# Mamba layers and a routed mixture of experts on one Trainium2 core: an expert plan cut into small pieces, the lead search moved to the last unit, and a state product put ahead of a transpose

## The chip, the core and the metric

One core of a Trainium2 chip. TensorE multiplies and transposes, VectorE, ScalarE and GpSimd do the elementwise work, SyncE issues most transfers. Each engine runs its own list of instructions in order; semaphores tie the lists together. The metric is the device time of one execution in microseconds.

## What is computed

Two Mamba2 layers on 8 sequences of 512 tokens of 256 features, a residual and a layernorm, then a mixture of 8 experts (2 per token), a residual and a layernorm. All in float32:

```python
for i in range(2):                                   # _mamba2, per layer
    res = h
    u = layernorm(h, ln_w[i], ln_b[i])
    z, xBC, dt = split(u @ in_w.T)
    dt = softplus(dt + dt_bias)
    xBC = silu(causal_conv(xBC, 4 taps) + conv_b)
    # scan over tokens, 8 heads, state 64 x 64:
    #   state = exp(dt*A)*state + (dt*x) B^T ;  y = state C
    y = (y + D * x) * silu(z)
    y = y * rsqrt(mean(y*y) + eps) * rms_w
    h = y @ out_w.T + res
x = layernorm(x + h)
logits = x @ gate_w + gate_b                         # top 2 of 8, softmax
for e: out_e = (silu(x @ w1g[e] + b1g) * (x @ w1v[e] + b1v)) @ w2[e] + b2[e]
x = layernorm(x + sum_of_two(out_e * weight))
```

## The kernel before, in words

**Units.** A unit is one sequence in one layer; units 0 to 15 follow each other (layer 0 is 0 to 7, layer 1 is 8 to 15). Each is worked in four chunks of 128 tokens. `schedule` (L142) calls, for each engine, a function with its order written out by hand: `prologue`, `first`, `plain` for units 1 to 8, `routed` for 9 to 14 (unit u also routes the tokens of sequence u - 9, whose layers ended a unit before), `final` for unit 15 and `epilogue`. Units 10 to 13 are two turns of a loop of two.

For a chunk TensorE does, among others: `chunk_cb` (C times B), `chunk_y` (the part of y within the chunk, L794, sixteen records), `chunk_z` (the old state times C, L781), `chunk_s` (the new state, L803), `chunk_c` (transposes of the gated g, L812) and `chunk_d` (output product, L830). `do_fills` puts the projections of the next unit between them. g comes from GpSimd (`gated`, L2506), which needs VectorE's `chunk_b2` (L1703), which needs `chunk_y`. `chunk_z` of chunk 1 needs ScalarE's `first_state` (L1278). VectorE's share is `scan` (L1676), `chunk_mix` (L1684), the taps of the convolution (L1637), `g_low` (L1610), the sum of layer output and residual `end_add` (L1660), and the routing (`s3_stats`, `s3_top`, `s3_place`).

**Lead search.** Each token's row is scattered by GpSimd (L2456) to a queue per expert in DRAM. `choose_lead` (L1841, eleven small VectorE instructions, each waiting for the one before) picks the expert that has most rows after six sequences. Its 6 first tiles (`NLEAD`) are worked before the counts are complete. It is issued in unit 14, behind `s3_place`. GpSimd's `first_weights` waits for it and loads that expert's 3 MB in four quarters; ScalarE (L1289) and VectorE (L2062) split them into two halves of float16.

**Expert tiles.** 71 tiles of 128 rows, in groups of three. Per tile TensorE turns the rows (`turn`, L1054, two transposes), makes four banks of 24 products (L1076: gate and value of half 0, of half 1) and the result (L1101, 24 products) of the tile before; its order is turn of tile j + 2, banks of tile j + 1, result of tile j. ScalarE takes the gate's silu (L1520) and a high part (L1526). VectorE's tile is `rows_low` (L2044), then per half `gated` (L2232) and `low_part` (L2239), with `weigh_rows` (L2052, L2055) in between; `result` of the tile before (L2263) follows the tile. `turn` of tile j waits for its rows and for `rows_low` of tile j - 1. SyncE loads rows of tile j + 3 (L518 for the first six tiles, L572 after) behind the answer of tile j - 1 (L578), that is behind VectorE's `result`. From tile 6 on, the address of the rows comes from the plan, so SyncE waits for `plan_done`.

**Plan.** VectorE counts tiles per expert (`plan_tiles`, L2119 to L2132), finds which expert each tile has (`plan_places`, L2136 to L2148), and packs words and addresses (`plan_words`, L2155 to L2173; its last cast raises `plan_done`). `step` makes the engine wait for each instruction before the next. `rows_moved` (L2177 on), `rows_of_pick` and others prepare the final gathers. They stand whole between tiles: `plan_tiles` behind tile 0, `plan_places` behind tile 1, `plan_words` behind tile 2, `rows_moved` behind tile 3.

**GpSimd behind the units.** For experts 1 to 7: `load_weights` (four quarters; those of expert 1 are issued at once, later ones one after another) and `split` (L2406 to L2408, fifteen instructions). It waits for `plan_done` ahead of the load of expert 2.

## Time and profile before

| | before |
|---|---|
| median of three runs | 1465.58 us (1463.50 to 1468.26) |
| profiled execution | 1464.89 us, of it 1462.9 us span |
| TensorE busy | 1309.9 us, 90% |
| VectorE busy | 1110.9 us, 76% |
| ScalarE, GpSimd busy | 797.7 and 802.3 us, 55% each |
| mean of what the transfers moved | 99 GB/s over the span |

Times in the rows are microseconds from the start of the span. A matmul's end is modelled, and matmuls overlap a little, so a group of a bank shows 1.52 us where the next begins after 1.36. The granted clock of TensorE has two levels here, 1.2 and 2.4 GHz; a mean between them tells of a stretch with both. An idle time in brackets stands with the engine that ended it, as the semaphores show.

### The profile page before, as it was taken

To read this page: it belongs to the slowest core of one execution; us is meant where nothing else is said; L and a number is where in the kernel's file an instruction comes from. 1 tells how busy PE (TensorE), PEld (TensorE's weight loads), DVE (VectorE), ACT (ScalarE), POOL (GpSimd) and SP (SyncE) were. 2 spreads that over 40 slices of the span, in tenths; PEclk is the share of its full clock that TensorE was granted. 3 is DMA by queue.
4 is the path that set the end of the run, shared out by engine and by line. 5 is a ranking of instruction groups with operands and counts; after the bars stand their busy time and mean duration, and the time that the engine had idled before them with its cause. 6 is when DMAs were issued, how large, how long until landed. Compare 5 with 4: busy or idle time off the path is not lost.

```text
span 1462.9 us, 39961 instructions
## 1 busy us (share of the span) xinstructions
PE 1309.9 (90%) x13112; PEld 1038.5 (71%) x13113; DVE 1110.9 (76%) x2564; ACT 797.7 (55%) x1821; POOL 802.3 (55%) x738
## 2 busy tenths in 40 slices
PE   3889999999999999999888699999999999999970
PEld 1456665656666566566657589999999999999970
DVE  4889999999999898899877976656565656565537
ACT  4657666666576566566545245444444444444434
POOL 3466767766776777687775601506061607152771
PEclk9999999999999899899867899999999999999985
DMA  5313443223343233312415230212203222202594
GB/s 175 110 29 116 131 129 100 90 99 116 116 131 116 77 113 113 119 59 102 151 63 158 95 125 29 93 54 75 72 29 120 76 70 63 88 29 61 137 204 150
DMA packets 94655, 145.72 MB, mean 100 GB/s; under 512 B 13488, under 2 KB 77488, under 8 KB 94448
## 3 DMA queue, kind: packets, MB, share of 16 engines
q1 hardware_dynamic: 79216, 97.06, 21.0%
q0 software_dynamic: 15072, 46.51, 10.7%
q10 hardware_dynamic: 288, 1.19, 0.2%
q8 instruction: 39, 0.64, 0.2%
q14 instruction: 40, 0.33, 0.1%
HBM read 103.06 MB, written 41.67 MB: 99 GB/s over the span
## 4 chain that ended last, share of the span: by engine, by line
PE 58%; DVE 19%; issue 9%; POOL 8%; ACT 4%; DMA 1%; SPq 1%; DVEq 0%; ACTq 0%; POOLq 0%
PE pe L1076 13%; PE pa L1076 12%; PE py L1101 12%; PE pa L659 4%; DVE arena L1637 3%; POOL arena L2506 3%; PE pm L830 3%; PE pa L651 3%; PE py L794 3%; DVE arena L1676 2%; PE pz L781 2%; PE pt L812 2%; DVE arena L1684 1%; DVE arena L1703 1%; POOL arena L2496 1%
## 5 line engine op out<-in xcount | busy, mean ns | idle before, releaser
L1076 PE MATMUL pe<-arena 128*128 128x128 f16 x3408 | 222.9, 222 | 19.4 <-issue 17.4
L1076 PEld LDWEIGHTS pe<-arena 128*128 128x128 f16 x3408 | 207.2, 99 | 24.3 <-issue 21.4
L1076 PE MATMUL pa<-arena 128*128 128x128 f16 x3408 | 219.4, 220 | 2.1 <-issue 2.1
L1520 ACT ACTIVATE arena<-pe,arena 128x128 f32<-128x128 f32 x568 | 162.1, 371 | 83.4 <-PE pe L1076 81.9
L1076 PEld LDWEIGHTS pa<-arena 128*128 128x128 f16 x3408 | 201.9, 98 | 2.2 <-issue 2.2
L1101 PE MATMUL py<-arena 128*128 (+1 forms) x1704 | 197.5, 273 | 0.8 <-DVE arena L2263 0.8
L1637 DVE SCALAR_TENSOR_TENSOR arena<-pa,arena 128x511 f32<-128x511 f32 (+2 forms) x240 | 178.7, 745 | 8.1 <-ACT arena L1172 1.8
L1101 PEld LDWEIGHTS py<-arena 128*128 128x128 f16 x1704 | 163.5, 98 | 18.8 <-issue 1.1
L2406 POOL TENSOR_SCALAR arena<-arena 128x1536 f16<-128x1536 f32 (+2 forms) x35 | 42.7, 1220 | 216.2 <-DVE arena L2263 202.6
L2232 DVE SCALAR_TENSOR_TENSOR pm<-pa,arena 128x128 f32<-128x128 f32 x284 | 80.4, 352 | 98.0 <-ACT arena L1520 85.0
L794 PEld LDWEIGHTS py<-arena 128*128 128x128 f32 x1024 | 128.7, 202 | 35.5 <-issue 21.8
L1676 DVE TENSOR_TENSOR_SCAN arena<-arena,pe 128x512 f32<-128x512 f32 x128 | 148.7, 1203 | 3.4 <-issue 2.0
L794 PE MATMUL py<-arena 128*128 128x64 f32 x1024 | 133.8, 287 | 0.6 <-DVE arena L1684 0.6
L651 PE MATMUL pa<-arena 128*128 128x512 f16 x480 | 120.5, 391 | 3.6 <-DVE arena L1637 2.4
L2506 POOL TENSOR_TENSOR arena<-arena 128x512 f32<-128x512 f32 x64 | 88.7, 1386 | 63.0 <-DVE arena L1703 62.8
L1526 ACT ACTIVATE arena<-pm 128x512 f16<-128x512 f32 x71 | 42.4, 597 | 131.3 <-DVE pm L2232 131.3
L830 PE MATMUL pm<-arena 128*128 128x256 f16 x768 | 103.0, 288 | 8.6 <-DVE arena L1610 8.1
L2232 DVE SCALAR_TENSOR_TENSOR pz<-pa,arena 128x128 f32<-128x128 f32 x284 | 80.4, 351 | 39.6 <-ACT arena L1520 38.6
L1526 ACT ACTIVATE arena<-pz 128x512 f16<-128x512 f32 x71 | 42.4, 597 | 109.6 <-DVE pz L2232 109.6
L830 PEld LDWEIGHTS pm<-arena 128*128 128x128 f16 x768 | 78.3, 104 | 32.2 <-DVE arena L1610 10.1
L659 PE MATMUL pa<-arena 128*128 128x512 f16 x384 | 97.3, 396 | 4.2 <-ACT arena L1161 2.0
L2676 POOL DMA_INDIRECT arena<-answer,arena x64 | 61.6, 963 | 57.9 <-issue 57.6
(297 smaller groups left out, 2557.8 us busy)
## 6 DMA issues: line engine op xcount, KB each, us to landing
arena<-step_rows SPq DMA_DIRECT2D x64, 512.0 KB, 6.3
arena<-in_w_exp POOLq DMA_DIRECT2D x32, 768.0 KB, 4.7
arena<-queue SPq DMA_DIRECT2D x74, 129.5 KB, 2.1
answer<-arena SPq DMA_DIRECT2D x71, 128.0 KB, 1.7
arena<-in_x SPq DMA_DIRECT2D x16, 512.0 KB, 6.7
answer<-zeros SPq DMA_DIRECT2D x10, 512.0 KB, 4.8
arena<-h SPq DMA_DIRECT2D x9, 512.0 KB, 6.3
h<-arena SPq DMA_DIRECT2D x8, 512.0 KB, 3.0
```

The lines of the kernel that those rows point to most:

```text
L651: ins = pe.matmul(bank[:, :], win[:, l, b, d, OX + c * P:OX + (c + 1) * P], uT[:, vq, a, d, :], start=(n == 0), stop=(n == len(passes) - 1))
L659: ins = pe.matmul(bank[:, :], uT[:, vq, a, d, k * P:(k + 1) * P], win[:, l, b, d, 0:DI], start=(n == 0), stop=(n == len(passes) - 1))
L794: ins = pe.matmul(py[:, h * HD:(h + 1) * HD], mix[:, kq, h, :], dtx[:, kq, h, :], start=True, stop=True)
L830: ins = pe.matmul(OUT, gT[:, c.kq, a, t, :], wout[:, c.layer, b, t, :], start=(n == 0), stop=(n == len(passes) - 1))
L1076: ins = pe.matmul(bank[:, f * P:(f + 1) * P], w_split[:, p, hl, d * 2 * FF + col:d * 2 * FF + col + P], x[:, r, d, :], start=(n == 0), sto ...
L1101: ins = pe.matmul(py[:, 0:D], a[:, b, f, :], part(p, hl, W1N + f * D, D), start=(half == 0 and n == 0), stop=(half == 1 and n == len(passe ...
L1520: ins = e.activation(sg[:, half, f, :], GATE[half][:, f * P:(f + 1) * P], ACT.Silu, bias=b1a[:, bass.ds(ex_, 1), ff], scale=1.0 / S1)
L1526: e.activation(acth[:, r, 4 * half:4 * half + 4].rearrange("p f t -> p (f t)"), GLU[half][:, :], ACT.Copy).then_inc(hi_done[half], 1)
L1637: ins = dve.scalar_tensor_tensor(acc[:, mq, s:T], pa[bank][:, 0:T - s], cw[:, l, ct, TAPS - 1 - s:TAPS - s], acc[:, mq, s:T], ALU.mult, AL ...
L1676: dve.tensor_tensor_scan(flat[:, h * T:(h + 1) * T], step_b[:, c.k, h * T:(h + 1) * T], IDENT4[:, :], 0.0, ALU.mult, ALU.add).then_inc(sca ...
L2232: ins = dve.scalar_tensor_tensor(GLU[half][:, f * P:(f + 1) * P], VALUE[half][:, f * P:(f + 1) * P], b1v[:, bass.ds(ex_, 1), ff], sg[:, ha ...
L2506: pool.tensor_tensor(g[:, kq], y2[:, kq], zs[:, c.q, k].rearrange("p (h d) -> p h d", h=NH), ALU.mult).then_inc(g_ready, 1)
```

## The change

Four edits.

1. In `routed`, TensorE issues `chunk_z` of chunk 1 ahead of `chunk_c` of chunk 0 (six units).
2. VectorE issues `choose_lead` in `final` behind `chunk_mix` of chunk 1 and ahead of `end_add`, no longer in unit 14. In GpSimd's `final`, `first_weights` and the first scatter come behind `gated`, `x_w`, `x_dt` and `old_state`, no longer in front.
3. The plan's three functions become ten, with the same instructions in the same order but for one (`row_f` is made a little earlier). They stand between the halves of a tile or between tiles, from tile 0 to tile 4, and the last, `plan_out`, behind the result of tile 3. What follows (`rows_moved`, picks, needs) comes two tiles later, and VectorE's loop starts at group 4 instead of 3.
4. GpSimd waits for `plan_done` behind the load of expert 1 and ahead of its split; the four quarters of expert 1 are issued one after another.

```diff
@@ TensorE, routed @@
                 chunk_cb(c[2])
+                chunk_z(c[1])
                 chunk_c(c[0])
-                chunk_z(c[1])
                 chunk_y(c[1])
@@ VectorE, routed @@
                 s3_place(st, ch3)
-                if isinstance(st.u, int) and st.u == NB + BEFORE_LEAD:
-                    choose_lead()
                 scan(c[4])
@@ VectorE, final @@
                 chunk_mix(c[1])
+                choose_lead()
                 end_add(st)
@@ VectorE, the plan @@
-            def plan_tiles():
+            def count_tiles():
...
+            def tiles_by_place():
...
+            def ends_of_places():
...
-            def plan_places():
+            def places():
...
+            def experts_of_tiles():
...
+            def starts_of_tiles():
...
+            def parities():
...
-            def plan_words():
+            def words():
...
+            def rows_of_tiles():
...
+            def plan_out():
...
+                step(dve.tensor_reduce(plan_f[0:1, 3 * NJT + 2 * NE:], usedj[0:1, 0:NJ].rearrange("p (g r) -> p r g", r=WB),
+                                       AX.X, ALU.add))
                 dve.tensor_copy(plan_i[0:1, :], plan_f[0:1, :]).then_inc(plan_done, 1)
@@ VectorE, tiles @@
+            def first_half(i, r, ex_, expert):
+                rows_low(i, r + 1)
+                gated(i, r, 0, ex_)
+                weigh_rows(i, r + 1, expert)
+                low_part(i, r, 0)
+
+            def second_half(i, r, ex_):
+                gated(i, r, 1, ex_)
+                low_part(i, r, 1)
@@ VectorE, order @@
-            tile(0, 0, first, lead[:, 0:1])
-            plan_tiles()
-            tile(0, 1, first, lead[:, 0:1])
+            first_half(0, 0, first, mine)
+            count_tiles()
+            second_half(0, 0, first)
+            tiles_by_place()
+            first_half(0, 1, first, mine)
+            ends_of_places()
+            second_half(0, 1, first)
             result(0, 0, True)
-            plan_places()
-            tile(0, 2, first, lead[:, 0:1])
+            places()
+            first_half(0, 2, first, mine)
+            experts_of_tiles()
+            second_half(0, 2, first)
             result(0, 1, True)
-            plan_words()
-            tile(1, 0, first, lead[:, 0:1])
+            starts_of_tiles()
+            first_half(1, 0, first, mine)
+            parities()
+            second_half(1, 0, first)
             result(0, 2, True)
+            words()
+            first_half(1, 1, first, mine)
+            rows_of_tiles()
+            second_half(1, 1, first)
+            result(1, 0, False)
+            plan_out()
+            first_half(1, 2, first, e_tab[:, NLEAD:NLEAD + 1])
+            second_half(1, 2, first)
+            result(1, 1, False)
             rows_moved()
...
-            with dve.Fori(3, NGRP) as i:
+            with dve.Fori(4, NGRP) as i:
@@ GpSimd, load_weights @@
-                    if n > 0 and e > 1:
+                    if n > 0 and e > 0:
                         pool.wait_ge(w_raw_in, 16 * (4 * e + n))
@@ GpSimd, final @@
                 end(st)
-                first_weights()
-                scatter_before(st, 0, 1)
                 gated(c[0])
                 x_w(c[1])
                 x_dt(c[1])
                 old_state(c[1])
+                first_weights()
+                scatter_before(st, 0, 1)
                 scatter_before(st, 1, 3)
@@ GpSimd, behind the units @@
                     pool.wait_ge(w_have, 1)
-                if e == 2:
+                load_weights(e)
+                if e == 1:
                     pool.wait_ge(plan_done, 1)
-                load_weights(e)
```

## Rows read from the trace of the kernel before

**Rows 1.** The page: TensorE's granted clock in 40 slices, tenths of 2.4 GHz
```profile
PEclk9999999999999899899867899999999999999985
```

**Rows 2.** Windows of two routed units: busy time and count, clock, DMA
```profile
485.37:537.26 51.89, 49.71 (x294) 32.63 (x293) 43.39 (x110) 31.18 (x63) 37.00 (x37) 0.87 0.32 103
...
636.69:683.62 46.93, 44.84 (x294) 29.99 (x293) 43.23 (x110) 31.17 (x63) 37.05 (x37) 0.96 0.30 101
```

**Rows 3.** Timeline of TensorE, units 10, 12, 14: start, us, instruction, [idle before, releaser]
```profile
487.06 0.65 PE L812 MATMUL pt<-ident,arena 128*128 128x128 f32 x4 [1.20 <-POOL arena L2506]
487.64 2.07 PE L781 MATMUL pz<-arena 64*128 64x512 f32 x2
...
588.31 1.11 PE L812 MATMUL pt<-ident,arena 128*128 128x128 f32 x4 [3.64 <-POOL arena L2506]
...
685.77 1.12 PE L781 MATMUL pz<-arena 64*128 64x512 f32 x2
```

**Rows 4.** Timeline of VectorE, the lead search and the last unit's sum
```profile
716.93 1.04 DVE L1850 TENSOR_TENSOR lead_score<-count,qbase 128x8 f32<-128x8 f32 x1
...
721.94 0.17 DVE L1860 CAST at_pos<-lead_pos 128x8 int32<-128x8 f32 x1
...
737.25 1.57 DVE L1660 TENSOR_TENSOR arena<-arena 128x1024 f32<-128x1024 f32 x1 [3.32 <-ACT arena L1240]
```

**Rows 5.** Timeline of TensorE, last output product of unit 14
```profile
724.99 2.74 PE L830 MATMUL pm<-arena 128*128 128x256 f16 x12 [5.78 <-DVE arena L1610]
```

**Rows 6.** Windows, four microseconds in the last unit
```profile
728.00:732.00 4.00, 4.00 (x20) 3.67 (x20) 1.18 (x2) 0.15 (x1) 0.15 (x1) 0.50 1.02 419
```

**Rows 7.** Timeline of TensorE, turns of rows (L1054) and a first bank, early tiles
```profile
815.71 0.66 PE L1054 MATMUL pt<-ident,arena 128*128 128x128 f32 x2 [4.46 <-DMA arena<-queue]
816.16 2.72 PE L1076 MATMUL pe<-arena 128*128 128x128 f16 x24
...
835.52 0.66 PE L1054 MATMUL pt<-ident,arena 128*128 128x128 f32 x2 [9.94 <-issue]
...
847.52 0.41 PE L1054 MATMUL pt<-ident,arena 128*128 128x128 f32 x2 [1.82 <-DMA arena<-queue]
...
856.55 0.38 PE L1054 MATMUL pt<-ident,arena 128*128 128x128 f32 x2
...
864.83 0.38 PE L1054 MATMUL pt<-ident,arena 128*128 128x128 f32 x2
```

**Rows 8.** Timeline of VectorE, plan functions (L2119, L2136, L2155 to L2173) and tiles (L2044)
```profile
796.49 0.34 DVE L2119 TENSOR_SCALAR arena<-jrow 128x32 f32<-128x32 f32 x1
...
800.77 0.42 DVE L2044 TENSOR_TENSOR arena<-pt,arena 128x256 f16<-128x256 f32 x1
...
806.84 0.78 DVE L2136 TENSOR_TENSOR arena<-jrow,arena 128x600 f32<-128x600 f32 x1
...
812.72 0.42 DVE L2044 TENSOR_TENSOR arena<-pt,arena 128x256 f16<-128x256 f32 x1
...
818.78 2.95 DVE L2155 COPY arena<-arena 1x25 f32<-1x25 f32 x1
...
833.82 1.27 DVE L2173 CAST arena<-arena 1x244 int32<-1x244 f32 x1
```

**Rows 9.** Timeline of SyncE's DMA issues, early tiles
```profile
807.57 0.35 SPq L518 DMA_DIRECT2D arena<-queue  x1
...
843.20 0.35 SPq L572 DMA_DIRECT2D arena<-queue  x1
```

**Rows 10.** Timeline of GpSimd, last unit and split of expert 1
```profile
723.79 2.30 POOL L2390 DMA_DIRECT2D arena<-in_w_exp  x4 [1.22 <-issue]
...
747.00 0.20 POOL L2446 TENSOR_TENSOR arena<-arena 128x4 f32<-128x4 f32 x1
...
818.60 3.10 POOL L2408 TENSOR_TENSOR arena<-arena 128x1536 f16<-128x1536 f32 x1
```

**Rows 11.** Timeline of ScalarE, split of expert 0's weights (high parts)
```profile
756.72 1.48 ACT L1289 ACTIVATE arena<-arena 128x1536 f16<-128x1536 f32 x1
```

More of the change, by code:

```diff
@@ L2115, in _ @@
             par_f = plan_f[0:1, 2 * NJT:3 * NJT]
-            def plan_tiles():
+            NG = NJT // WB
+            number, odd = pos_j[0:1].rearrange("p (g r) -> p g r", r=WB), ej[0:1].rearrange("p (g r) -> p g r", r=WB)
+            packed = par_f[:, 0:NG]
+            def count_tiles():
                 step(dve.tensor_scalar(j128, jrow[:, 0:NTILE], float(P), None, ALU.mult))
@@ L2166, in plan_words @@
                 dve.tensor_copy(plan_f[0:1, 3 * NJT + NE:3 * NJT + 2 * NE], end[0:1, :])
+                step(dve.tensor_tensor(row_f, tmpj[0:1], jd, ALU.add))
+            def plan_out():
                 step(dve.tensor_tensor(usedj[0:1, 0:NJ], jrow[0:1, 0:NJ], end[0:1, NE - 2:NE - 1].to_broadcast([1, NJ]),
                                        ALU.is_lt))
[L2170 to L2172 removed]
+                step(dve.tensor_reduce(plan_f[0:1, 3 * NJT + 2 * NE:], usedj[0:1, 0:NJ].rearrange("p (g r) -> p r g", r=WB),
+                                       AX.X, ALU.add))
                 dve.tensor_copy(plan_i[0:1, :], plan_f[0:1, :]).then_inc(plan_done, 1)
@@ L2241, in low_part @@
                                   ALU.subtract).then_inc(act_done, 1)
-            def tile(i, r, ex_, expert):
-                rows_low(i, r + 1)
-                for half in range(2):
-                    gated(i, r, half, ex_)
-                    if half == 0:
-                        weigh_rows(i, r + 1, expert)
-                    low_part(i, r, half)
+            def first_half(i, r, ex_, expert):
[6 more added lines that the diff above has]
+                low_part(i, r, 1)
+            def tile(i, r, ex_, expert):
+                first_half(i, r, ex_, expert)
+                second_half(i, r, ex_)
             def planned(i, r):
```

25 lines of the change are left out of this document (11 added, 14 removed).

## The prediction

> **What bounds the kernel now.** I read the page first for where TensorE is not at full clock: slices 14 and 17, 20 to 23, and the last two [rows 1]. The last two are the tail, which the change doesn't touch. So I read three stretches: the routed units (430 to 720 us), the last unit (720 to 783), and the first expert tiles (783 to 858).
>
> Routed units, each measured from its `chunk_cb` of chunk 2: unit 13 (636.69 to 683.62) lasts 46.93 us, VectorE busy 43.23 and TensorE 44.84; unit 10 lasts 51.89 [rows 2]. Both engines are near full, so what one gains the other may take back. In all six routed units TensorE waits over 1 us for GpSimd's g ahead of the transposes L812. In units 10 and 12 that wait (1.20 and 3.64 us) is followed by half clock: the state product L781 takes 2.07 us where it takes 1.12 in unit 14 [rows 3].
>
> Last unit: the search for the leading expert stands in VectorE's order ahead of unit 14's last scan. It starts at 716.93 and its last step ends at 722.11: 5.2 us for eleven tiny steps [rows 4]. TensorE idles 5.78 us behind it, comes back at 1.2 GHz [rows 5] and stays there though it is busy, 4.00 us of 4.00 in 728 to 732 at 0.50 [rows 6].
>
> Early tiles: TensorE waits 4.46, 9.94 and 1.82 us ahead of its turns of tiles 4, 5 and 6 [rows 7]. The first is for rows whose load was issued at 807.57 and used at 815.71 [rows 7, 9]; the second for VectorE, which sits in `plan_words` from 818.78 to 835.09 [rows 8]; the third for a load issued at 843.20 [rows 9]. In steady state a tile costs TensorE 8.28 us, turn to turn [rows 7], and VectorE 6.07 (800.77 to 806.84) [rows 8]. From there on the program is TensorE's, and answers, gathers and the final normalisation follow counts of tiles, so a time saved before that is saved at the end.
>
> **Part 1, state product ahead of the transposes (six units).** The product needs only `first_state`, long done when TensorE stands waiting. At full clock its 1.05 us (1.12 less overlap) fits into the waits; the transposes start no later. In units 9, 11, 13 and 14, however, TensorE later waits for VectorE's taps anyway, so it hands back what it won; I take 0, bounds 0 and 1 us for the four. Unit 10 is 51.89 - 46.93 = 5.0 us longer than unit 13 [rows 2]. If the filled wait keeps the clock, all of it comes back; if the clock falls all the same, the path is still shorter by one product at half rate, 2.0. I take 4.0. In unit 12 a wait of 3.64 - 1.05 = 2.6 us is left, so the clock falls as before, and the product is off the path: 2.0, less what VectorE's order takes; 1.5. A fall could also move to another place, where it costs 3 to 5 us, so the bounds are -3 and 8. Part 1: 5.5 us.
>
> **Part 2, the search moved.** In unit 14 the 5.2 us go from in front of the scan, so `g_low` of chunk 3 is ready at about 719.8 and TensorE idles 0.8 us, as much as in the units before (0.3 to 1.0). Then its clock should hold. Its work from 724.99 to the end of the state's product at 734.5 is 9.5 us without a wait at half clock, so 4.7 at full: that product ends near 725.0. ScalarE's first state, rows and scaling (3.2 us) let `end_add` begin near 728 instead of 737.25 [rows 4]. Now the search stands right in front of it, behind `chunk_mix` of chunk 1, which ends near 725.2. There VectorE waited 3.32 us for ScalarE before [rows 4]; of the search's 2 to 5 us some 2.8 are hidden, and it sets `end_add` back by 0 to 2.4, taken as 1.3. VectorE would be some 8 us ahead.
>
> GpSimd has more to do in that stretch. Its issue of expert 0's weights (723.79, 2.30 us) [rows 10] and the scatter behind it lay in idle time. Now they stand behind the old state, in the middle of work without a gap: x_w at 726.1, three products to 729.2, weights to 731.8, three scatters to 735.7, two products to 738.1, then the root at 739.4 instead of 747.2 [rows 10]: 7.8 ahead. That is the chain which the trace shows critical in this unit, so GpSimd's 7.8 counts, not VectorE's 8. The weights land about 8.4 us after their last issue, near 740; ScalarE's split of the first quarter began at 756.72 [rows 11], so near 748 after: hidden by 8 us. If the clock stays at half, only the 5.2 less the search's new 1.3 remains, about 3.5. I take 7.5, bounds 1 and 9.
>
> **Part 3, the plan in ten pieces.** The same instructions are issued, with one wait more. Until the plan is handed out VectorE has 4.3 us (796.49 to 800.77), 5.9 (806.84 to 812.72) and `plan_words`, whose 15 instructions took 16.3 us [rows 8]. The first two show such steps at 0.2 to 0.3 each, so 3.8 is the size of the third alone. What makes it 16.3: a copy of 1x25 lasts 2.95 us [rows 8], until a GpSimd subtraction begun at 818.60 ends [rows 10]; GpSimd splits expert 1 just then. The change keeps the split back until the plan is out, so the plan is 4.3 + 5.9 + 3.8 = 14.0 us. The Trainium skill ("SBUF — State Buffer", on its doors and the shared port pair) says that a GpSimd operation and a VectorE operation that is in a two-port mode or has two SBUF inputs exclude each other for the whole instruction. By that rule taken literally the sum would be rival A's below; these two rows agree with it.
>
> When is the plan out? VectorE leaves tile 0 at 796.49 [rows 8], then 14.0 of plan and four tiles of 6.07: 834.8, less 1 us of ScalarE waits that pieces between halves cover: 834. Before it was 835.09. So the plan is out no sooner; but tile 4 is done by then, where tile 2's result was open.
>
> TensorE: turn 3 as before. Turn 4's rows need `result(0,0)`, behind the same 4.3 us, so they are issued at 807; their 8.1 us fell among four weight quarters in flight at once, now one at a time, and the load at 843.20, beside single quarters, took 4.2 [rows 7, 9]. So turn 4 near 811.4, waiting 0 to 0.5 (4 if it stays 8.1). Turn 5 waits for VectorE's lag, about 0.6. Turn 6 is asked for at 811.4 + 0.6 + 2 x 8.28 = 828.6, and gets its rows only from the plan: 834 + 1.3 (SyncE's waits and address) + 2.6 (a load beside no weights, issued at 800.11 and used at 802.78) = 837.9. That is a new wait of 9.3 us, for plan, SyncE and DMA. The clock falls; the first bank behind such a gap took 2.72 for 1.52 [rows 7], and with a second and the turn that is 1.6. Old turn 6: 847.52 at full clock. Gain: 847.5 - 837.9 - 1.6 = 8.0.
>
> Given back: expert 1's split (25.5 us) ran from 815.5 and now runs from 834 to 860, over `rows_moved` and the first `rows_of_pick`. At the rate of `plan_words` (1.09 us an instruction) `rows_moved`'s eight cost 8.7 instead of 1.5. VectorE has 2.2 us of slack a tile and had just been waiting for TensorE at turn 6, so of these 7 us TensorE sees some 1; bounds 0 and 7. TensorE needs expert 1 at tile 11, after 885. Part 3: 7.0, bounds 1 and 9.
>
> Sum: 5.5 + 7.5 + 7.0 = 20.0. The profiled execution took 1464.89 (span 1462.9 and 2.0 around it), 0.7 under the median 1465.58. 1465.6 - 20.0 = **1445.6**.
>
> **The rivals.**
> - A, the lock moves with the split. For this rival every blockable step of `rows_moved` (seven of eight) and of the first pick (three of four) waits for a whole GpSimd instruction. For: the copy of 2.95 us [rows 8]. Against: 15 steps passed in the time of 10 GpSimd instructions, so half the time two pass at one boundary. Part 3 gives 1: 1451.6. Chance 0.20.
> - B, VectorE and GpSimd take the gain of the units. Clock falls only move, and the last unit stays at 1.2 GHz. For: 43.2 of 46.9 us busy [rows 2]. Part 1 gives 0, part 2 gives 3.5: 1465.6 - 10.5 = 1455.1. Chance 0.14.
> - C, both: 1 + 3.5 + 0: 1461.1, within 0.3%. Chance 0.09.
> - D, slower: after turn 6's wait the clock does not come back for several tiles (tiles 5 to 8). For: 1.2 GHz held with TensorE busy 4.00 of 4.00 us [rows 6]. Against: after waits of 4.46 and 9.94 it came back within two banks. A tile at half clock costs 8.3 more; from 2.4 tiles on the 20 us are gone, four give 1465.6 - 20 + 33 = 1479. Chance 0.06.
> - E, the change does not do what it says for the search: another expert leads, or first weights come late. Against: the search sees the same counts (unit 14's are the last added at both places), and the margin is 8 us. Time as without part 2: 1453.1. Chance 0.03.
>
> **How the numbers follow.** Forecast 0.48, its own range 1441 to 1450. A, B and E are faster too. About 0.3% (4.4 us) is what a measurement can tell from no change. Faster: 0.48 + 0.20 + 0.14 + 0.03 = 0.85, of which 0.02 moves to same, as B adjoins it: 0.83. Same: 0.09 + 0.02 = 0.11. Slower: 0.06. Range: from 1439 (all three parts at their upper bounds, 26 us, is 1439.6) to 1460, which takes in A, B and E and leaves out C and D, 0.15, and an edge of B.
>
> **What would show it.** Right: 722 to 747 at full clock and the root near 739; no wait over 2 us at turns 4 and 5, one of 8 to 10 us at turn 6, ended by a load issued just after the plan's last cast; expert 1's split starting at that cast and `rows_moved` stretched; unit 10 near 47 us. Wrong: turn 4 still waiting 4 us (the quarters were not its cause); unit 10 at 52; TensorE waiting behind `rows_moved` for over 3 us.

## The result and the profile after

| | before | after |
|---|---|---|
| median | 1465.71 us (1463.50 to 1468.26, four runs) | 1444.99 us (1442.04 to 1445.83, four runs) |
| ratio | | 0.9854, 95% interval 0.9833 to 0.9876 |
| profiled execution | 1464.89, span 1462.9 | 1445.83, span 1443.9 |
| TensorE busy | 1309.9 | 1300.4 |
| VectorE busy | 1110.9 | 1098.9 |

1445.6 was forecast. The page of the changed kernel, TensorE's granted clock in 40 slices:

```profile
PEclk9999999999999999999967999999999999999985
```

Against [rows 1], slices 14 and 17 are at full clock now; the dip in the last unit is still there, as 6 and 7 in slices 21 and 22.

To place the difference I cut both traces at the same instructions: the first `steps` product of units 9 and 14 (L764, weights `tri_le`), the first bank of tile 0, and the turns of tiles 10 and 13.

| stretch | before | after | gain | forecast |
|---|---|---|---|---|
| start to unit 9 | 437.71 | 439.88 | -2.2 | 0 |
| units 9 to 13 | 245.13 | 233.15 | 12.0 | 5.5, with unit 14 |
| unit 14 and last unit, to tile 0's first bank | 100.23 | 98.27 | 2.0 | 7.5 |
| tile 0's first bank to turn 10 | 99.29 | 92.36 | 6.9 | 7.0 |
| the rest | 580.5 | 580.2 | 0.3 | 0 |

The sum is 19.0, the difference of the spans, for a forecast of 20.0. So the total is right, and two of its terms are not. The first line is code that the change leaves alone; the last section returns to it.

**Units.** The windows of all five units, before and then after (columns as in [rows 2]):

```profile
437.71:682.84 245.13, 231.60 (x1467) 154.37 (x1466) 217.46 (x547) 156.05 (x310) 179.66 (x175) 0.93 0.31 101
```

```profile
439.88:673.03 233.15, 219.52 (x1467) 148.55 (x1466) 216.62 (x547) 156.50 (x310) 179.48 (x175) 0.98 0.33 107
```

TensorE is busy 12.1 us less at a clock of 0.98 for 0.93, and its idle time is the same (13.5 and 13.6 us). By estimate from these two clocks, 17 us of full-speed work were lost to half clock before and 5 after, which is the whole 12. VectorE is busy only 0.8 us less, so VectorE's gain must be waits. Its waits in those units before (who waited, for whom: us in all, times, longest):

```profile
DVE arena L1710 <- PE pz L803: 6.1, 5, 3.4
DVE pe L1813 <- PE pa L704: 4.4, 4, 1.3
...
DVE arena L1703 <- PE py L794: 1.8, 2, 0.9
DVE arena L1690 <- PE pz L781: 1.4, 2, 0.7
```

It had waited for TensorE too: for the new state (L1710), for the ranks of the routing (L1813), for the chunk's products. Of these 13.7 us, 9.9 lie in units 10 and 12; units 9, 11 and 13 have 1.5, 1.1 and 1.2, nearly all of it for the ranks. The prediction took VectorE as an engine that TensorE waits for in these units, not the other way round.

Units 9, 11 and 13 were not undisturbed before, either: each has a stretch of some 3 us at half clock. Unit 13 before, that stretch of it, and unit 13 after:

```profile
635.90:682.84 46.94, 44.85 (x295) 30.00 (x294) 43.24 (x111) 31.18 (x62) 36.94 (x36) 0.96 0.30 101
662.00:664.00 2.00, 2.00 (x8) 0.83 (x7) 2.00 (x4) 0.60 (x1) 1.70 (x3) 0.50 1.02 382
```

```profile
627.38:673.03 45.65, 43.09 (x295) 29.04 (x294) 43.21 (x111) 31.38 (x62) 36.85 (x36) 1.00 0.31 105
```

**Last unit.** TensorE, VectorE and GpSimd of the changed kernel, timeline (start, us, engine, line, instruction, [idle before, releaser]):

```profile
710.64 1.47 PE L830 MATMUL pm<-arena 128*128 128x256 f16 x12 [0.31 <-ACT arena L1232]
...
731.11 2.07 PE L781 MATMUL pz<-arena 64*128 64x512 f32 x2 [4.21 <-DVE arena L1710]
733.11 3.58 PE L692 MATMUL pa<-arena 128*128 128x8 f32 x16
...
739.47 3.68 PE L794 MATMUL py<-arena 128*128 128x64 f32 x16
```

```profile
729.77 0.69 DVE L1703 TENSOR_TENSOR arena<-py,arena 128x512 f32<-128x512 f32 x1 [1.44 <-POOL arena L2542]
730.38 0.67 DVE L1710 TENSOR_TENSOR arena<-pz,arena 64x512 f32<-64x512 f32 x1
```

```profile
720.93 2.28 POOL L2436 DMA_DIRECT2D arena<-in_w_exp  x4
723.52 1.05 POOL L2502 DMA_INDIRECT queue<-arena  x1 [0.30 <-issue]
...
726.19 0.96 POOL L2502 DMA_INDIRECT queue<-arena  x1 [0.31 <-issue]
727.17 1.05 POOL L2530 TENSOR_TENSOR arena<-arena 128x512 f32<-128x512 f32 x1
728.38 1.26 POOL L2542 TENSOR_TENSOR arena<-arena 128x512 f32<-128x512 f32 x1 [0.15 <-POOL arena L2530]
...
730.73 0.20 POOL L2492 TENSOR_TENSOR arena<-arena 128x4 f32<-128x4 f32 x1
```

The wait of 5.78 us in [rows 5] is 0.31 us now, the clock is full up to 727, and the root's last step stands at 730.73, counted from unit 14's start 6.5 us ahead of its old place in [rows 10] (7.8 forecast). Up to the last output product of unit 14 (L830, 710.64) this is a gain of 4.5 us, 37.6 for 42.2. But the weights and three scatters (720.93 to 727.2) now stand ahead of x*d and its sum (727.17 to 729.6). VectorE's `chunk_b2` of chunk 1 (L1703) waits 1.44 us for that sum, the new state (L1710) is behind it, and TensorE waits 4.21 us for the state. From L830 to tile 0's first bank TensorE takes 60.7 us for 58.1 before, so 2.6 of the 4.5 are lost again. TensorE is back at half clock, with L781 at 2.07 and L794 at 3.68 us, busy all the time:

```profile
731.00:745.00 14.00, 13.89 (x46) 9.54 (x46) 5.05 (x7) 4.14 (x9) 8.59 (x8) 0.50 0.21 78
```

**Early tiles.** TensorE's turns 5 and 6 (L1054) and the banks behind turn 6; then two of VectorE's steps of the plan, its last among them, and SyncE's load for tile 6:

```profile
809.08 0.41 PE L1054 MATMUL pt<-ident,arena 128*128 128x128 f32 x2 [1.30 <-DMA arena<-queue]
...
823.72 0.66 PE L1054 MATMUL pt<-ident,arena 128*128 128x128 f32 x2 [6.18 <-DMA arena<-queue]
824.17 2.77 PE L1076 MATMUL pe<-arena 128*128 128x128 f16 x24
826.73 1.97 PE L1076 MATMUL pa<-arena 128*128 128x128 f16 x24
```

```profile
811.37 0.15 DVE L2170 COPY arena<-arena 1x25 f32<-1x25 f32 x1
...
820.17 0.28 DVE L2193 CAST arena<-arena 1x244 int32<-1x244 f32 x1
```

```profile
821.55 0.35 SPq L572 DMA_DIRECT2D arena<-queue  x1
```

The waits of 4.46 and 9.94 us at turns 4 and 5 in [rows 7] are 0 and 1.30, and the one at turn 6 is 6.18 for 1.82. The copy of 1x25 that took 2.95 us in [rows 8] takes 0.15.

### The profile page after: what moved, and what is told of

The parts are those of the page before. It is cut to its first block, busy times and chain, and to the rows that moved or that the text cites. A ratio compares the mean times of both kernels' runs of the same rounds, so it can differ in the third digit from the quotient of the medians.

```text
span 1443.9 us, 39948 instructions
## 1 busy us (share of the span) xinstructions
PE 1300.4 (90%) x13112; PEld 1033.6 (72%) x13113; DVE 1098.9 (76%) x2564; ACT 797.2 (55%) x1821; POOL 801.1 (55%) x738
## 3 DMA queue, kind: packets, MB, share of 16 engines
q0 software_dynamic: 15072, 46.51, 11.0%
## 4 chain that ended last, share of the span: by engine, by line
PE 54%; DVE 21%; issue 10%; POOL 7%; ACT 3%; DMA 1%; SPq 1%; DVEq 1%; POOLq 0%; ACTq 0%
PE pe L1076 12%; PE pa L1076 12%; PE py L1101 11%; DVE arena L1637 3%; PE pa L659 3%; POOL arena L2552 3%; DVE arena L1676 3%; PE pa L651 3%; PE py L794 2%; PE pm L830 2%; PE pt L812 2%; PE pz L781 1%; DVE arena L1703 1%; DMA arena<-queue 1%; DVE arena L1684 1%
## 5 line engine op out<-in xcount | busy, mean ns | idle before, releaser
L1076 PE MATMUL pe<-arena 128*128 128x128 f16 x3408 | 222.1, 222 | 18.2 <-issue 17.2
L1076 PEld LDWEIGHTS pe<-arena 128*128 128x128 f16 x3408 | 206.1, 99 | 23.5 <-issue 21.7
L1076 PE MATMUL pa<-arena 128*128 128x128 f16 x3408 | 219.7, 220 | 2.2 <-issue 2.0
L1076 PEld LDWEIGHTS pa<-arena 128*128 128x128 f16 x3408 | 202.2, 98 | 2.5 <-issue 2.1
L794 PEld LDWEIGHTS py<-arena 128*128 128x128 f32 x1024 | 125.8, 199 | 30.2 <-issue 16.0
L794 PE MATMUL py<-arena 128*128 128x64 f32 x1024 | 130.3, 282 | 0.9 <-DVE arena L1684 0.9
L830 PE MATMUL pm<-arena 128*128 128x256 f16 x768 | 98.0, 279 | 5.1 <-DVE arena L1610 4.6
L830 PEld LDWEIGHTS pm<-arena 128*128 128x128 f16 x768 | 75.7, 101 | 26.6 <-issue 8.2
```

The source lines that it names most:

```text
L794: ins = pe.matmul(py[:, h * HD:(h + 1) * HD], mix[:, kq, h, :], dtx[:, kq, h, :], start=True, stop=True)
L830: ins = pe.matmul(OUT, gT[:, c.kq, a, t, :], wout[:, c.layer, b, t, :], start=(n == 0), stop=(n == len(passes) - 1))
L1076: ins = pe.matmul(bank[:, f * P:(f + 1) * P], w_split[:, p, hl, d * 2 * FF + col:d * 2 * FF + col + P], x[:, r, d, :], start=(n == 0), sto ...
```

## The experiments

Six kernels take one part alone or take one part out, two change what the trace pointed to, the last four ran side by side: the changed kernel again and three more. In the table "units" is 9 to 13, "last" from unit 14 to tile 0's first bank, "tiles" from there to the turn of tile 13 (the expectations call it turn 12, counting from the turn behind that first bank as zero; their other turns are named as here). The three stretches come from one profiled execution of each, the medians from several. Kernels p1 to p4 ran on one chip, where before had 1470.76; a1, a2, b1 and b2 on another (1473.18), the last four on a third (1468.44). The kernel before ran from 1462 to 1480 us in its 40 executions there, the longer ones at a lower mean clock (0.94 for 0.95), so a median can differ from before by more than two profiles do: p1_swap by 14.8 us in the medians and by 8.9 in the profiled spans.

| kernel | units | last | tiles | median | ratio to before, 95% |
|---|---|---|---|---|---|
| before | 245.1 | 100.2 | 124.9 | 1465.71 | |
| after | 233.2 | 98.3 | 118.0 | 1444.99 | 0.985 (0.983 to 0.988) |
| p1_swap | 233.0 | 102.1 | 125.3 | 1455.98 | 0.988 (0.984 to 0.993) |
| p2_lead | 246.2 | 97.9 | 122.6 | 1464.49 | 0.997 (0.993 to 1.000) |
| p3_plan | 246.2 | 107.6 | 118.6 | 1467.61 | 0.997 (0.994 to 1.000) |
| p4_hold | 245.1 | 100.3 | 117.7 | 1462.42 | 0.994 (0.991 to 0.998) |
| a1_free_split | 231.8 | 98.5 | 129.3 | 1456.57 | 0.990 (0.985 to 0.995) |
| a2_quarters | 232.1 | 98.3 | 122.0 | 1447.33 | 0.982 (0.976 to 0.987) |
| b1_pool_order | 231.8 | 94.7 | 119.7 | 1443.95 | 0.981 (0.976 to 0.986) |
| b2_rows_first | 231.8 | 98.1 | 118.6 | 1440.86 | 0.978 (0.973 to 0.983) |
| after_again | 233.1 | 99.3 | 119.2 | 1444.81 | 0.983 (0.978 to 0.987) |
| b3_order_again | 232.5 | 94.1 | 119.1 | 1443.49 | 0.983 (0.979 to 0.987) |
| b4_both | 233.1 | 96.1 | 115.4 | 1439.53 | 0.980 (0.976 to 0.985) |
| c1_whole_plan | 233.1 | 98.0 | 117.5 | 1441.98 | 0.981 (0.977 to 0.985) |

Behind the turn of tile 13 all fourteen profiles take the same, 554.2 to 556.0 us to the end of the span: the prediction's ground that "a time saved before that is saved at the end" holds.

### The exchange in the routed units alone: p1_swap

```diff
@@ TensorE, routed, on the kernel before @@
                 chunk_cb(c[2])
+                chunk_z(c[1])
                 chunk_c(c[0])
-                chunk_z(c[1])
                 chunk_y(c[1])
```

> The kernel before with one edit: in the routed units the state product of the second chunk goes ahead of the transposes of g. Everything else is as before. Theory (the routed units keep what TensorE's wait gave up, because VectorE was waiting for TensorE's ranks in each unit too): units 9 to 13 together are about 12 us shorter, the time falls by 10 to 13 us. Rival (the term of the prediction: VectorE takes it back, only the two disturbed units gain): 5.5 us, units 9, 11 and 13 as long as before (46.9 us).

Measured: 1455.98 for 1470.76, a little more than the 10 to 13 us expected, and units 9 to 13 took 232.95 us for 245.13: 44.94, 46.51, 45.66, 50.22 and 45.62 each. All five are shorter, those that took 46.9 before by 1.3 to 1.9. VectorE's waits in them, in the same view:

```profile
DVE arena L1710 <- PE pz L803: 2.1, 1, 2.1
...
DVE pe L1813 <- PE pa L704: 1.2, 1, 1.2
```

They fell from 6.1 and 4.4 us to 2.1 and 1.2, and the two for L1703 and L1690 (1.8 and 1.4) are off the list, whose least is 0.5: some 10 of the 12.2 us. The last stretch was 1.9 us longer than before; unit 14 up to its last output product took 42.1 us as before, so it has no share. The rival, that VectorE takes the gain back, falls. The exchange is over half of the whole change.

How much of it is order and how much clock can be told from all profiles. In the four kernels without the exchange (before, p2_lead, p3_plan, p4_hold) none of the twenty units 9 to 13 has a granted clock of 1.00; in the ten profiles with it 34 of 50 have. At the same clock of 0.96 unit 9 took 46.9 us without it and 46.2 with it (after_again), unit 13 46.9 and 46.3 (b3_order_again); at 1.00 they take 44.9 and 45.6. So against the 46.9 us of before, 0.6 to 0.7 come at the same mean clock, and another 0.7 to 1.3 where no half clock is left. That the order is what keeps the clock is shown by this count; why it fell where it did is not.

### The search moved alone: p2_lead

```diff
@@ VectorE, routed, on the kernel before @@
                 s3_place(st, ch3)
-                if isinstance(st.u, int) and st.u == NB + BEFORE_LEAD:
-                    choose_lead()
@@ VectorE, final @@
                 chunk_mix(c[1])
+                choose_lead()
                 end_add(st)
@@ GpSimd, final @@
-                first_weights()
-                scatter_before(st, 0, 1)
                 gated(c[0])
                 x_w(c[1])
                 x_dt(c[1])
                 old_state(c[1])
+                first_weights()
+                scatter_before(st, 0, 1)
```

> The kernel before with one edit: the leading expert is sought in the last unit, and GpSimd issues the weights and the first scatter behind the products of the old state. Theory: TensorE's wait of 5.8 us before the transposed decays goes, but VectorE's second half of chunk 1 waits for GpSimd's add of x*d, TensorE then waits over 3 us for the next state and runs its next banks at half clock: the time falls by 1 to 3 us only. Rival (the prediction's term): 7.5 us.

Measured: ratio 0.9965, some 5 us, for 1 to 3 expected and 7.5 by the rival; but the stretch that the edit touches gained only 2.3 (97.92 for 100.23: 5.0 won up to unit 14's last output product, 2.7 lost behind it), and another 2.3 came in the tiles, where turn 4 already stood 2.0 us nearer to tile 0's first bank (30.7 for 32.6). The same sum holds up VectorE again, by the same time, and TensorE waits 1.69 us for the state, where over 3 were expected, with half clock behind it:

```profile
738.80 0.69 DVE L1703 TENSOR_TENSOR arena<-py,arena 128x512 f32<-128x512 f32 x1 [1.44 <-POOL arena L2495]
739.41 0.67 DVE L1710 TENSOR_TENSOR arena<-pz,arena 64x512 f32<-64x512 f32 x1
```

```profile
740.13 2.07 PE L781 MATMUL pz<-arena 64*128 64x512 f32 x2 [1.69 <-DVE arena L1710]
```

The forecast 7.5 for this part is refuted. The wait for the sum of x*d comes with the edit. Half clock came once ahead of it too (L830 took 2.77 us at 733.55), which in after it did not.

### The plan's part alone: p3_plan

```diff
@@ on the changed kernel: the exchange and the search undone @@
-                chunk_z(c[1])
                 chunk_c(c[0])
+                chunk_z(c[1])
...
+                if isinstance(st.u, int) and st.u == NB + BEFORE_LEAD:
+                    choose_lead()
                 scan(c[4])
...
```

> The changed kernel with the two other parts undone: the plan in pieces, the split of expert 1 held until the plan is done, the quarters one by one; routed units and the search as before. Theory, and the prediction's term: the stretch from the first bank of tile 0 to the turn of tile 10 is about 7 us shorter than before (93.5 to 95 us for 99), and the time falls by 6.5 to 7.5 us. If the three parts are not independent (the later start of the tiles moves the loads), it falls by less than 5 or more than 9.

Measured: the tiles did what was expected, 92.8 us from the first bank to turn 10 for 99.3, so 6.5. Yet the median fell by 3.2 only, by the ratio 4.7. The difference is in the stretch ahead of the tiles, which the kernel has word for word as before: 107.57 us for 100.23. Of these 7.3 us, 5.5 came in unit 14. Its wait of 1.08 us for g, as long as before, was followed by half clock here, as in unit 10 in [rows 3]; before, L781 at this place took 1.12 us:

```profile
685.60 2.04 PE L781 MATMUL pz<-arena 64*128 64x512 f32 x2
687.57 3.67 PE L794 MATMUL py<-arena 128*128 128x64 f32 x16
...
730.35 2.74 PE L830 MATMUL pm<-arena 128*128 128x256 f16 x12 [4.85 <-DVE arena L1610]
```

From unit 14's start to that last product, this kernel and then before:

```profile
682.66:730.35 47.69, 41.36 (x223) 26.97 (x221) 39.59 (x110) 25.73 (x51) 33.28 (x33) 0.85 0.24 81
```

```profile
682.84:724.99 42.15, 34.87 (x223) 23.64 (x221) 39.99 (x110) 25.75 (x51) 33.17 (x34) 0.98 0.29 92
```

Behind it 1.8 us more came, at a clock of 0.64 for 0.68. Why the clock fell in unit 14 this time is not settled. What is shown: the same code in the same order costs 7 us more or less by where the clock is low.

### The split held, the plan uncut: p4_hold

```diff
@@ GpSimd, on the kernel before @@
-                    if n > 0 and e > 1:
+                    if n > 0 and e > 0:
...
-                if e == 2:
-                    pool.wait_ge(plan_done, 1)
                 load_weights(e)
+                if e == 1:
+                    pool.wait_ge(plan_done, 1)
```

> The kernel before with one edit: the split of expert 1 on GpSimd is held until the plan is done, and the quarters of expert 1 are started one by one; the plan is not cut. If GpSimd's split is what stretched the plan's small steps (the 1x25 copy of 2.95 us beside a pass of the split of 3.10 us), the steps of the words take 0.15 to 0.4 us, the plan's cast ends 8 to 12 us earlier than in the kernel before, and this alone gives 4 to 8 us of part 3. Rival: what counts is the cut of the plan; then the time is within 2 us of before, because the whole plan still stands between two casts of rows and TensorE waits at turns 5 and 6 as before.

Measured: tiles 117.7 us, 7.2 less than before and as good as after (118.0), so the rival, that the cut is what counts, falls. The words and the cast, whole, between two tiles:

```profile
820.89 0.16 DVE L2155 COPY arena<-arena 1x25 f32<-1x25 f32 x1
...
823.50 0.24 DVE L2170 TENSOR_REDUCE arena<-arena 1x3 f32<-1x72 f32 x1
...
823.92 0.28 DVE L2173 CAST arena<-arena 1x244 int32<-1x244 f32 x1
```

They ran from 820.89 to 824.20, in 3.3 us, where they took 16.3 in [rows 8] and the prediction had 3.8. The cast stands 38.7 us behind tile 0's first bank; in the changed kernel it is 48.9, in the kernel before 50.8. So the held split and the single quarters give the whole gain of this part, and the cut puts the cast back by ten.

### The changed kernel with the split free: a1_free_split

```diff
@@ GpSimd, on the changed kernel @@
+                if e == 2:
+                    pool.wait_ge(plan_done, 1)
                 load_weights(e)
-                if e == 1:
-                    pool.wait_ge(plan_done, 1)
```

> The changed kernel with one part undone: the split of expert 1 isn't held until the plan is done, so it runs beside the pieces of the plan. Theory (held split is what keeps the plan's small steps short): single steps of the words take 1 to 3 us again, the cast comes 4 to 9 us later than in the changed kernel, TensorE waits 10 to 15 us at turn 6 instead of 6.2, and the time is 3 to 8 us above the changed kernel. Rival (the pieces are spread so widely that the split costs nothing): within 1 us of it.

Measured: tiles 129.3 us, 11.3 more than after and 4.4 more than before. The cut and the single quarters without the held split are a loss: TensorE waits 17.58 us at turn 6, above the 10 to 15 expected, and the span is 8.7 us longer than after's, for 3 to 8. VectorE's steps, with GpSimd's instructions in the same microseconds:

```profile
822.60 1.02 DVE L2184 COPY arena<-arena 1x8 f32<-1x8 f32 x1
...
827.35 0.99 DVE L2193 CAST arena<-arena 1x244 int32<-1x244 f32 x1
```

```profile
822.56 1.04 POOL L2453 TENSOR_SCALAR arena<-arena 128x1024 f32<-128x1024 f32 x1
...
827.05 1.15 POOL L2454 TENSOR_TENSOR arena<-arena 128x512 f16<-128x512 f32 x1
```

The copy of eight elements ends at 823.62, with GpSimd's pass begun at 822.56; it took 0.16 with no split about. The cast took 0.99 for 0.28, and ended with the subtraction begun at 827.05. The Trainium skill ("SBUF — State Buffer", on the shared port pair) says that a GpSimd instruction which holds the pair keeps out for its whole length a VectorE instruction that wants it; those ends agree, to 0.02 and 0.14 us. GpSimd's spans are rough, so no more can be read from them. Not every step was held: the reduction ahead of the cast took 0.24 us beside the split too.

### The quarters at once: a2_quarters

```diff
@@ on the changed kernel @@
-                    if n > 0 and e > 0:
+                    if n > 0 and e > 1:
```

> The changed kernel with one part undone: the four quarters of expert 1's second matrix are started at once. Theory: the row loads of tiles 4 and 5 land later beside them, TensorE waits 3 to 6 us more at these turns (0.0 and 1.3 in the changed kernel), of which turn 6 takes back nothing because the plan's steps follow the tiles: 2 to 5 us above the changed kernel. Rival (turn 6 hangs on the plan alone and swallows the waits ahead of it): within 1 us.

Measured: tiles 122.0 us for 118.0 and 119.2 in the two executions of after, so 2.8 to 4.0 more; the median is 2.3 to 2.5 above after's, but on another chip, and by the ratio to before the two do not differ (0.982 for 0.985 and 0.983), so for the whole time this is not shown. Turn 4 waits 2.19 us where it waited 0, turn 5 not at all, and turn 6 stands 55.2 us behind tile 0's first bank, for 52.4 and 53.4. Starting the quarters one by one is worth some 3 us of the tiles in these profiles; that they were the cause of turn 4's wait stands, though not all of its 4.46.

### GpSimd's order in the last unit: b1_pool_order

```diff
@@ GpSimd, final, on the changed kernel @@
                 old_state(c[1])
-                first_weights()
-                scatter_before(st, 0, 1)
-                scatter_before(st, 1, 3)
                 x_d(c[1])
                 add_xd(c[1])
+                first_weights()
                 rsqrt_x1(st)
-                scatter_before(st, 3, 4)
+                scatter_before(st, 0, 4)
```

> The changed kernel with GpSimd's order in the last unit changed: x*d and its add for chunk 1 go ahead of the issue of the weights and of the scatters. Theory (this add is what VectorE's second half of chunk 1 waited 1.44 us for, TensorE 4.21 us for the next state behind it, and then the clock fell to half): TensorE's wait shrinks below 2.5 us or goes, the clock stays full to the first tile, the first bank of tile 0 comes 4 to 7 us earlier and the time is 3 to 6 us below the changed kernel. Rival (another input sets that wait, VectorE's own work ahead of it): the wait moves to the next input, and the gain is under 1.5 us.

Measured: the last stretch took 94.7 us for 98.3 (the median is 1.0 below after's, on another chip), and VectorE no longer waits for the sum (L1703 at 722.30 has no idle time ahead of it). TensorE:

```profile
715.46 1.97 PE L674 MATMUL pa<-ident,arena 128*128 128x128 f32 x8 [1.28 <-DVE arena L1660]
...
726.30 1.12 PE L781 MATMUL pz<-arena 64*128 64x512 f32 x2 [0.36 <-DVE arena L1710]
...
731.67 1.12 PE L812 MATMUL pt<-ident,arena 128*128 128x128 f32 x4 [1.55 <-POOL arena L2552]
```

The wait for the state is 0.36, for 4.21. A fall of the clock came all the same, but earlier (L674 took 1.97 us at 715.46): 0.51 from 715 to 725, 0.91 to 729, 0.50 to 735 and 0.84 to 745, by windows of this run. The 44 us ahead of tile 0 were at 0.69, for 0.59. So the cause named for the wait is right, and the stretch is 3.6 us shorter here; the next kernel, with the same order, did not keep that. That the clock would stay full to the first tile was wrong. Behind it a new wait of 1.55 us for GpSimd's gated product shows.

### The row numbers first: b2_rows_first

```diff
@@ VectorE and SyncE, on b1_pool_order @@
+            def rows_out_first():
+                dve.tensor_copy(plan_i[0:1, 0:NJT], row_f).then_inc(rows_known, 1)
...
             starts_of_tiles()
             first_half(1, 0, first, mine)
-            parities()
+            rows_of_tiles()
             second_half(1, 0, first)
+            rows_out_first()
             result(0, 2, True)
-            words()
             first_half(1, 1, first, mine)
-            rows_of_tiles()
+            parities()
             second_half(1, 1, first)
             result(1, 0, False)
+            words()
             plan_out()
+            rows_moved()
...
             result(1, 1, False)
-            rows_moved()
...
-            sp.wait_ge(plan_done, 1)
+            sp.wait_ge(rows_known, 1)
```

> The kernel of the run before this one, and the plan's row numbers are worked out ahead of its words: they are cast in the pass of tile 3, with a semaphore of their own for SyncE's loads, and the parities, the words and the moved rows follow. Theory: the load for tile 6 no longer waits for the last cast (821.55 in the changed kernel), and TensorE's wait of 6.2 us at turn 6 shrinks to 0 to 3 us: 3 to 6 us below the run before. Rival: the parities and words behind it make the split and the weights of expert 1 late, and the gain is back by turn 10: within 1 us of the run before.

Measured: the median is 3.1 us below b1's, of four runs each, and the intervals overlap. The wait at turn 6 went altogether, and turn 7 stood 59.8 us behind tile 0's first bank, for 63.1 in b1. By turn 13 1.0 us of the 3.3 was left. TensorE's idle times behind turn 6:

```profile
819.90 2.74 PE L1077 MATMUL pe<-arena 128*128 128x128 f16 x24 [2.28 <-issue]
...
845.88 0.41 PE L1055 MATMUL pt<-ident,arena 128*128 128x128 f32 x2 [1.30 <-DVE arena L2044]
...
866.38 0.41 PE L1055 MATMUL pt<-ident,arena 128*128 128x128 f32 x2 [1.57 <-DMA arena<-queue]
```

So at this place the wait for rows was first in a row of late things: a bank at 819.90 waited 2.28 us for a cause which the trace does not name and came back slow, and later turns waited for VectorE and for rows. The last unit took 98.1 us, for 94.7 in the same code of b1. It had gone into that stretch without b1's early fall, had its wait of 5.04 us for GpSimd's gated product, behind the weights and four scatters, and had half clock from there:

```profile
724.20 1.12 PE L782 MATMUL pz<-arena 64*128 64x512 f32 x2 [1.40 <-DVE arena L1711]
...
732.25 1.12 PE L813 MATMUL pt<-ident,arena 128*128 128x128 f32 x4 [5.04 <-POOL arena L2558]
```

### Four side by side

The changed kernel again:

> The changed kernel itself, unchanged, on the chip of the three runs beside it: it is what they are measured against. Expected 1444 to 1448 us, and the same three waits as in its first profile: over 4 us for the next state of chunk 1 in the last unit, about 6 us at turn 6, about 1.5 us at turn 9.

Measured: 1444.81, with waits of 4.21 us for the state, 5.79 at turn 6 and 1.58 at turn 9. Turn 3 waited 3.94 where it waited 0.80 in the first profile: these loads vary by some microseconds from one execution to the next.

The third order of GpSimd:

```diff
@@ GpSimd, final, on b1_pool_order @@
                 add_xd(c[1])
+                x_dt(c[2])
+                gated(c[1])
                 first_weights()
                 rsqrt_x1(st)
-                scatter_before(st, 0, 4)
-                x_dt(c[2])
-                gated(c[1])
                 x_w(c[2])
                 x_d(c[2])
                 old_state(c[2])
                 add_xd(c[2])
+                scatter_before(st, 0, 2)
                 gated(c[2])
...
```

> The changed kernel with GpSimd's last unit in a third order: x*d, its add, and also the gated product of chunk 1 go ahead of the issue of the weights, and the scatters go into GpSimd's idle time later. The first other order (add ahead, gated product behind) took the wait for the next state from 4.21 us to 0.36 and 1.40 us, but left one of 1.55 and 5.04 us for the gated product. Theory (GpSimd's queue in this stretch is the bound, and only an order that meets both dates gives the time): neither wait is over 1.5 us, the clock stays full to the first tile, tile 0's first bank comes 4 to 8 us earlier than in the changed kernel, counted from the last routed unit, and the time falls by 4 to 7 us. Rival (what the stretch lasts is set by whether the clock happens to be granted, or by VectorE): under 2 us.

Measured: the last stretch took 94.1 us for 99.3, so 5.2; the median fell by 1.3 only, less than these runs vary. No wait for GpSimd is left in 720 to 735, but one of 1.67 us for the state, and the clock fell behind that one too:

```profile
724.88 1.91 PE L781 MATMUL pz<-arena 64*128 64x512 f32 x2 [1.67 <-DVE arena L1710]
726.72 3.58 PE L692 MATMUL pa<-arena 128*128 128x8 f32 x16
```

Both theory and rival are half right. This stretch took 98.3 and 99.3 us in the two profiles of after, and 94.7, 98.1, 94.1 and 96.1 in the four with the sum ahead of the issues (b1, b2, b3, b4): the order is worth 0 to 5 us there, and the clock's fall no order of GpSimd removed.

The third order with the row numbers first:

> The kernel with the third order, with the plan's row numbers cast ahead of its words as in the earlier run of that edit, where the wait at turn 6 went (6.2 to 0 us) but waits and slow banks at turns 7 to 11 came in its place. Theory (the split and the tiles' own weights set the end of this stretch, not turn 6): the time from the first bank of tile 0 to turn 12 stays within 1 us of the kernel with the third order alone, and so does the whole. Rival (the waits behind it were chance): 3 us below it.

Measured: 1439.53, the lowest median of all, with tiles at 115.4 for 119.1. The rival is the nearer here, 3.7 us in the tiles, where b2 had kept 1.0 of such a gain over b1; so what the late split gives back stays open. Against after on the same chip it is 5.3 us, and the two intervals (0.976 to 0.985 and 0.978 to 0.987) overlap, so this is likely better and not shown.

All parts, but the plan uncut:

```diff
@@ on p4_hold: the exchange and the search as in p1_swap and p2_lead @@
```

> The kernel before with the exchange in the routed units, the search moved to the last unit and the split of expert 1 held until the plan is done, its quarters one by one, but with the plan in its old four blocks and not cut. Theory (the held split is what gave the time in the early tiles, the cut gave none): the stretch from tile 0's first bank to turn 12 lasts 117 to 119 us as in the changed kernel (117.95), and the whole is within 1.5 us of it. Rival (the cut gives the gain together with the later split): 4 to 7 us above the changed kernel.

Measured: 1441.98 for 1444.81, 2.8 below where 1.5 either way was expected, with overlapping intervals; tiles 117.5 for 119.2. The cast begins at 808.07, 38.8 us behind tile 0's first bank (769.32). TensorE then waits at turns 3 to 8 (1.77, 0.88, 2.09, 1.16, 0.51 and 3.33 us) where after has one long wait; two of them:

```profile
810.07 0.41 PE L1054 MATMUL pt<-ident,arena 128*128 128x128 f32 x2 [2.09 <-DMA arena<-queue]
...
841.70 0.41 PE L1054 MATMUL pt<-ident,arena 128*128 128x128 f32 x2 [3.33 <-DMA arena<-queue]
```

The rival, that the cut is what gives the gain, falls. Ten pieces, a changed loop and a second function for each half tile bring nothing that the moved wait does not bring alone.

## Why the prediction came out right, point by point

- **Part 1: 12.0 us for 5.5.** The step that failed is "TensorE later waits for VectorE's taps anyway, so it hands back what it won; I take 0". For unit 10, 4.0 were forecast and it gained 5.4 (51.89 to 46.53 between `steps`), unit 12 gained 2.1 for 1.5; those two were a little under-sized. But units 9, 11 and 13 gained 1.9, 1.3 and 1.3 where 0 stood, 4.5 in all, and the bound of 1 us for four units was too low as well. Before, TensorE waited 0.3 us for the taps in each of them (L674), and VectorE waited 0.9 to 1.3 us for TensorE's ranks; with the exchange TensorE's wait for taps is 1.1 to 1.2 us, so it does hand something back, and the one for the ranks is gone. Nor was unit 13 the undisturbed measure that it was taken for: its clock is 0.96 in [rows 2], and that stretch at half clock went too (p1_swap has the shares). A busy share near full (43.2 of 46.9 us) had been taken for an engine that waits for no one. The rival B, by which VectorE and GpSimd take the gain, falls with it.
- **Part 2: 2.0 us for 7.5.** What is asked of VectorE and the search came as written: the search took 3.0 us (715.93 to 718.96), the wait of 5.78 went, the root moved by 6.5 for 7.8. The failed step is "That is the chain which the trace shows critical in this unit, so GpSimd's 7.8 counts". The prediction had counted the weights and scatters ahead of "two products to 738.1", and saw only what stands behind them on GpSimd, the root. It did not ask who waits for those two products: VectorE's second half of chunk 1 does, TensorE's state behind it, and there the clock fell (4.21 us and L781 at 2.07 us). With the sum ahead of the issues the stretch gives back 3.6 and 5.2 us in b1_pool_order and b3_order_again, but 3.2 in b4_both and 0.2 in b2_rows_first. So the wait is the cause of a part of the missing 5.5; how large a part changes with the clock and is not settled. The bound of 1 us held.
- **Part 3: 6.9 us for 7.0, by the mechanism forecast, with two sizes off that cancel.** Turn 4 waits for nothing (0 to 0.5 forecast), turn 5 1.30 for 0.6, turn 6 stands 52.4 us behind tile 0's first bank for 54.8, and its wait is 6.2 for 9.3, because the cast was done at 49.2 for 50.9. Behind the slow banks, at turn 7, the gain was 10.3 for 8.0. The load was issued 1.1 us behind the cast and used 2.2 later (1.3 and 2.6 forecast), the next banks took 2.77 and 1.97. The split began at 820.55, at the cast's end; `rows_moved` took 5.0 us for 8.7 forecast and 1.5 before, and TensorE's waits behind it were 0.2 to 0.4 us, 1.35 for rows at turn 9, and 0.3 and 0.8 behind that. By turn 10, 3.4 us were given back for 1 forecast; the waits add up to 3.3, which is the size that the prediction named as a sign of being wrong. That 6.9 meets 7.0 is luck. That the held split is the source is shown by a1_free_split against after, and by p4_hold and c1_whole_plan, where nothing else in the early tiles stands beside it but the single quarters (some 3 us by a2_quarters). The held split with the quarters at once and the plan whole was not tried. What the prediction did not ask is whether the cut has a share: it has none, or one below nothing.
- **The sum.** Part 1 gave 6.5 more and part 2 5.5 less than forecast, and the two cancel; the 2.2 us ahead of unit 9 work against both. That 1445.6 and 1444.99 lie 0.6 apart is chance. Rival A, the lock moved with the split, falls by turn 10 and by `rows_moved`; rival D, half clock for several tiles behind turn 6, by L1076 at 1.53 us from 829.11 on. C, with 1461.1, falls by the time, and E by ScalarE's split of the first weights, which began at 744.53 with no wait (near 748 forecast).

## What to carry to other kernels

- A busy share says nothing of who waits for whom. Before an engine is taken to hand a gain back, list its own waits in that stretch and their releasers: 13.7 us stood there for VectorE, with TensorE's name. And before a stretch is taken as the undisturbed measure, look at its clock: 0.96 was not 1.00.
- When instructions are moved forward in a queue past others, name the consumer of each instruction they are put ahead of, not only the last. Six microseconds of issues stood ahead of one sum, and 2.6 of the 4.5 us that the move had won were lost behind it.
- A small chain on one engine beside a long elementwise job on another can be cheap or dear by that neighbour alone. Try holding the neighbour back before cutting the chain up: here the moved wait, with the loads one by one, gave all of it.

## What the runs showed of the hardware

- With GpSimd's split about, several of VectorE's steps on a few dozen elements took 1 to 3 us each (2.95 for the copy of 1x25); without it 0.15 to 0.4. The word block and its cast took 16.3 us beside it and 3.3 without.
- TensorE stayed at 1.2 GHz with hardly a gap: busy 13.89 of 14.00 us at a granted clock of 0.50 (731 to 745 of after). Kernels with the same order in unit 14 and the last unit differed by 7 us in them (p4_hold 100.3, p3_plan 107.6), 5.5 of it in unit 14, at a granted clock of 0.98 and 0.85.
- The part ahead of unit 9, the same code in all fourteen profiles, took 436.4 to 439.9 us. So one profile against another says nothing of 3 us unless the stretch is named. What sets this spread stays open; the difference lies ahead of the `steps` product of unit 1 (it stands at 109.05 us in after, at 106.88 in before); from there to unit 9 all take the same to 0.2 us.
